# The first layer of a fused four-layer graph network: edge pieces and their products a turn apart, degree sums and first x tile ahead of turn 0

## What is computed

```python
h = maximum(layernorm(x), 0)
x = x + L0(h, W, adj, bias)   # diag, triu, tril of adj, each with its own W[k]
h = maximum(layernorm(x), 0)
x = x + L1(h, adj, ...)       # A_norm = adj + I; dinv = rsqrt(row + column sums - diagonal)
...                           # A_hat = A_norm * dinv[:, None] * dinv[None, :]
x = x + L2(...)               # two graph convolutions and LSTMs over windows
x = x + L3(h, ..., adj, src, dst)   # attention over 256 edges
```

## Time and profile before

| | |
|---|---|
| median of 3 runs | 1282.31 us |
| the profiled execution | 1282.6 us |
| its span | 1280.9 us |
| stage_first within the span | 0 to about 193 us |
| PE busy, share of the span | 95% |
| DVE, ACT, POOL busy | 79%, 68%, 26% |
| mean granted clock of PE | 0.993 |

### The profile page before, as it was taken

How to read it: one execution, slowest core, us unless ns; L and a number is a source line. 1 busy time by engine, 2 the same in 40 slices (tenths; PEclk the granted TensorE clock), 3 DMA queues, 4 the chain that set the end, 5 groups by cost and what they waited for, 6 DMA issues and landing times.

```text
span 1280.9 us, 22499 instructions
## 1 busy us (share of the span) xinstructions
PE 1223.2 (95%) x7286; PEld 1017.2 (79%) x7286; DVE 1013.9 (79%) x2032; ACT 870.9 (68%) x1657; POOL 333.9 (26%) x738
## 2 busy tenths in 40 slices
PE   4888999999899998899999999999999899999998
PEld 4888996663398887689778887888898777778998
DVE  4786868987768885988788878887886699988664
ACT  4564768868668886877687768777776577773332
POOL 4775761000067440000000000000000466653331
PEclk9998999999999999999999999999999999999999
DMA  8000000000031110000000000000200300001212
GB/s 307 1 1 2 2 1 1 0 1 0 19 122 66 66 58 1 1 1 2 1 1 1 1 1 1 1 1 27 105 2 1 132 1 1 2 1 41 75 67 83
DMA packets 14635, 38.22 MB, mean 30 GB/s; under 512 B 1872, under 2 KB 3920, under 8 KB 13392
## 3 DMA queue, kind: packets, MB, share of 16 engines
q1 hardware_dynamic: 13152, 36.31, 7.3%
q10 hardware_dynamic: 1392, 0.74, 0.2%
HBM read 20.27 MB, written 16.78 MB: 29 GB/s over the span
## 4 chain that ended last, share of the span: by engine, by line
PE 52%; DVE 5%; ACT 2%; issue 1%; POOL 1%; POOLq 0%; DVEq 0%; ACTq 0%
PE bank L1091 7%; PE bank L1092 7%; PE bank L1093 7%; PE bank L1563 4%; PE bank L1106 4%; PE bank L1357 4%; PE bank L1102 4%; PE bank L1103 4%; PE bank L1345 4%; PE bank L1553 2%; PE bank L1571 2%; ACT gates L1121 1%; PE bank L1329 1%; PE bank L1247 1%; DVE Y L1176 1%
## 5 line engine op out<-in xcount | busy, mean ns | idle before, releaser
L1121 ACT ACTIVATE gates<-bank,lstm_bias 128x512 f32<-128x512 f32 (+1 forms) x504 | 301.6, 636 | 102.1 <-PE bank L1106 89.2
L161 ACT ACTIVATE l_h<-X,nmr,rstd 128x128 f32<-128x128 f32 (+1 forms) x512 | 209.9, 483 | 38.6 <-POOLq L155 25.9
L1091 PE MATMUL bank<-lstm_node_hi,Wih_hi 128*128 128x512 f32 (+1 forms) x408 | 149.4, 366 | 0.0
L1092 PE MATMUL bank<-lstm_node_hi,Wih_lo 128*128 128x512 f32 (+1 forms) x408 | 148.9, 365 | 0.0
L1093 PE MATMUL bank<-lstm_node_lo,Wih_hi 128*128 128x512 f32 (+1 forms) x408 | 148.9, 365 | 0.0
L130 POOL TENSOR_TENSOR l2r_sum<-l2r_st 128x8 f32<-128x8 f32 x16 | 4.2, 263 | 529.1 <-DVE l2r_st L111 529.1
L1102 PE MATMUL bank<-lstm_hid_hi,Whh_hi 128*128 128x512 f32 (+1 forms) x288 | 104.5, 363 | 4.0 <-DVE lstm_hid_hi L1181 3.8
L1106 PE MATMUL bank<-lstm_hid_lo,Whh_hi 128*128 128x512 f32 (+1 forms) x288 | 106.9, 371 | 0.0
L1103 PE MATMUL bank<-lstm_hid_hi,Whh_lo 128*128 128x512 f32 (+1 forms) x288 | 103.2, 358 | 0.0
L1126 ACT ACTIVATE gates<-lstm_cell 128x512 f32<-128x512 f32 (+1 forms) x144 | 83.7, 581 | 20.8 <-DVE lstm_cell L1168 20.5
L1093 PEld LDWEIGHTS bank<-lstm_node_lo,Wih_hi 128*128 128x128 f32 x408 | 77.1, 189 | 11.6
(11 more groups left out here) (248 smaller groups left out, 3275.4 us busy)
## 6 DMA issues: line engine op xcount, KB each, us to landing
x_spill<-X SPq DMA_DIRECT2D x32, 256.0 KB, 2.0
X<-x_spill SPq DMA_DIRECT2D x2, 4096.0 KB, 12.6
out<-X SPq DMA_DIRECT2D x32, 256.0 KB, 2.0
X<-in_x SPq DMA_DIRECT2D x7, 1024.0 KB, 16.1
X<-in_x SPq DMA_DIRECT2D x2, 512.0 KB, 7.2
w_raw<-in_WihT SPq DMA_DIRECT2D x1, 1024.0 KB, 6.1
w_raw<-in_WhhT SPq DMA_DIRECT2D x1, 1024.0 KB, 8.3
W<-in_L_W ACTq DMA_DIRECT2D x1, 192.0 KB, 3.0
```

The costliest lines, as they stand in the source:

```text
L161: last = act.activation(h[:, j, :], k.X[:, bass.ds(b0, TB), :][:, j, :], ACT.Relu, bias=k.nmr[:, bass.ds(b0, TB)][:, j:j + 1], scale=k.rst ...
L1091: pe.matmul(out, hi, x_high, start=True, stop=False)
L1092: pe.matmul(out, lo, x_high, start=False, stop=False)
L1121: act.activation(gate_of(it, g), k.bank[4 * s + g][:, 0:it.N], ACT.Tanh if g == GATE_G else ACT.Sigmoid, bias=k.lstm_bias[:, it.p - 1, g:g ...
```

## The change

- **Edge pieces and products.** The constants change so that a full turn lies between each piece and its product: the scaled identity in behind(0) and the spread in turn 2; perm stays in behind(6) and the sort goes to turn 8; ST and DT in behind(8) and the adjacency product in turn 10; the three products behind it move by two turns as well. Copying the edge lists to float moves from turn 4 to turn 2 (READ), the rounded copy of DT to turn 9 (ROUND). PT, the four operations on Wqv and a_sign, and cont with reset are gathered behind turn 14 (REST).
- **Degree sums.** The seven DVE operations (L442 to L451) move from the end of turn 0 to a place ahead of turn 0; the pow for dinv on POOL moves from its turn 1 to a place between the coefficients of turns 0 and 1.
- **x first.** adj and adjT go to ACT's queue, ahead of the row vectors and W0; cols, W1T, W2T and Wg go from ACT's queue to SP's, behind x and the edge lists. x comes in pieces of 1, 1, 2, 2, 2 tiles and then six of 4.
- **First tile alone.** Turn 0's coefficients are made in two batches of one tile (4 columns) in place of one of 8; the counts that later waits look for grow by one.
- **Start of PE.** 8 dummy matmuls go before the diagonal product and 16 behind it; the waits for the split adjacency, for W0 and for the diagonal move from ahead of turn 0 into it, in front of their first use.

```diff
@@ LayerNormTail @@
     def wait(self, eng, s, turn):
-        eng.wait_ge(self.ready[s // self.per], turn + 1)
+        eng.wait_ge(self.ready[s // self.per], turn + 1 + (self.first_alone and (turn > 0 or s == 1)))
...
+    def coefficients_alone(self, pool, s):
+        self.batch(pool, 0, 0, s)
...
+        late = self.first_alone and (alone is None or alone == 1)
+        base = (turn * self.batches + q + late) * self.GROUPS
...
@@ stage_first @@
-    turns_in = [1, 1] + [2] * ((n_it - 2) // 2)
+    tiles_in = [1, 1, 2, 2, 2] + [4] * ((tiles - 8) // 4)
...
-    DEG, SPREAD, L3, FLOAT, RANK, PERM, SORTED, ADJ, SUM, TURN, SHARE = 0, 3, 3, 4, 5, 6, 7, 8, 9, 10, 11
+    SCALE, SPREAD, READ, FLOAT, RANK, PERM, SORTED, ROUND, ADJ, SUM, TURN, SHARE, REST = 0, 2, 2, 4, 5, 6, 8, 9, 10, 11, 12, 13, 14
@@ sync @@
-            sp.dma_start(adj[:, :], d["adj"]).then_inc(adj_in, 16)
-            sp.dma_start(k.adjT[:, :], d["adjT"]).then_inc(adj_in, 16)
...
+            sp.dma_start(k.cols[:, :], d["cols"]).then_inc(cols_in, 16)
+            sp.dma_start(k.W1T[:, :], d["W1T"]).then_inc(w_in, 16)
...
@@ gpsimd @@
-            x_ln.coefficients(pool, 0)
+            for s in range(S):
+                x_ln.coefficients_alone(pool, s)
+            pool.wait_ge(deg, 4)
+            pool.tensor_tensor(out=dinv[:, :], in0=rs[:, 3:4], in1=k.ln_const["-half"][:, 0:1], op=ALU.pow).then_inc(dinv_p, 1)
+            x_ln.coefficients(pool, 1)
             pool.iota(order_row[:, :], ...)
...
-            x_ln.coefficients(pool, 1)
@@ scalar @@
+            act.dma_start(adj[:, :], d["adj"]).then_inc(adj_in, 16)
+            act.dma_start(k.adjT[:, :], d["adjT"]).then_inc(adj_in, 16)
+            act.dma_start(k.rows[:, :, :], d["rows"].partition_broadcast(P)).then_inc(rows_in, 16)
             act.dma_start(W0[:, :, :], d["L0_W"].rearrange("k f o -> f k o")).then_inc(w0_in, 16)
...
-                if i == FLOAT:
+                if i == READ:
...
-                if i == ADJ:
+                if i == ROUND:
@@ tensor @@
             pe.wait_ge(cst, 2)
+            stay_awake(pe, k, psA[0], 8)
             pe.wait_ge(diag_in, 1)
             pe.matmul(spare[:, 0:P], k.ones[:, :], tmp[:, :], start=True, stop=True).then_inc(diag_done, 1)
-            pe.wait_ge(A_ready, 2)
-            pe.wait_ge(w0_in, 16)
+            stay_awake(pe, k, psA[0], 16)
...
@@ vector @@
-                if i == DEG:
...
-                if i == SPREAD - 1:
+                if i == SCALE:
...
-                if i == L3:
+                if i == REST:
+                    dve.tensor_tensor(e.PT[:, :], ST[:, :].bitcast(F32), DT[:, :], ALU.add)
                     dve.wait_ge(l3_in, 3 * 16)
...
-                    dve.wait_ge(matched, 2)
-                    dve.tensor_tensor(e.PT[:, :], ST[:, :].bitcast(F32), DT[:, :], ALU.add)
-                if i == SUM:
+                if i == REST:
                     chained(dve.memset(cont[:, :], 0.0))
...
-            x_stats(0)
+            x_stats(0, [0])
             dve.wait_ge(masks, 2)
             split_float32(dve, A12T[:, :, :], A_hi[:, :, :], A_lo[:, :, :], A_ready, 1).then_inc(A_ready, 1)
             dve.wait_ge(diag_done, 1)
             dve.tensor_copy(diag_bc[:, :], spare[:, 0:P]).then_inc(diag_done, 1)
-            x_stats(1)
-            for s in range(S):
-                h_low(0, s)
+            x_stats(0, [1])
+            degrees()
+            x_stats(1, [0])
+            h_low(0, 0)
+            x_stats(1, [1])
+            h_low(0, 1)
```

More of the change, by code:

```diff
@@ L118, in coefficients, with batch @@
             self.batch(pool, turn, q)
-    def batch(self, pool, turn, q):
+    def coefficients_alone(self, pool, s):
+        self.batch(pool, 0, 0, s)
+    def batch(self, pool, turn, q, alone=None):
         k, c = self.k, self.k.ln_const
[L122 to L126, removed]
+        whole, first = self.per * self.nb, (alone or 0) * self.nb
+        width = whole if alone is None else self.nb
+        st6 = self.st6[:, q * whole + first:q * whole + first + width, :]
+        su, di, m2 = self.sum[:, 0:width], self.diff[:, 0:width], self.m2[:, 0:width]
+        late = self.first_alone and (alone is None or alone == 1)
+        base = (turn * self.batches + q + late) * self.GROUPS
+        rows = bass.ds((turn * self.batches + q) * whole + first, width)
         rstd, nmr = k.rstd[:, rows], k.nmr[:, rows]
@@ L134, in group @@
             pool.sem_inc(self.tally, 1)
-        for s in range(q * self.per, (q + 1) * self.per):
+        for s in range(q * self.per, (q + 1) * self.per) if alone is None else [alone]:
             pool.wait_ge(self.stats_ready[s], turn + 1)
@@ L142, in batch @@
         group(1)
-        pool.sem_inc(self.stats_free[q], 1)
+        if alone is None or alone == self.per - 1:
+            pool.sem_inc(self.stats_free[q], 1)
         tt(di, di, di, ALU.mult)
@@ L197, in stage_first @@
     tile = lambda i, s: X[:, (i * S + s) * TB:(i * S + s + 1) * TB, :]
-    turns_in = [1, 1] + [2] * ((n_it - 2) // 2)
-    x_in = each(len(turns_in), lambda c: sem(f"x_in{c}"))
-    chunk_of = [c for c, n in enumerate(turns_in) for _ in range(n)]
+    tiles_in = [1, 1, 2, 2, 2] + [4] * ((tiles - 8) // 4)
+    x_in = each(len(tiles_in), lambda c: sem(f"x_in{c}"))
+    chunk_of = [c for c, n in enumerate(tiles_in) for _ in range(n)]
     adj_in, w0_in, w_in, rows_in, cols_in, edges_in, l3_in = (
@@ L234, in _ @@
         def _(sp):
-            sp.dma_start(adj[:, :], d["adj"]).then_inc(adj_in, 16)
-            sp.dma_start(k.adjT[:, :], d["adjT"]).then_inc(adj_in, 16)
             first = 0
-            for c, n in enumerate(turns_in):
-                rows = slice(first * S * TB, (first + n) * S * TB)
+            for c, n in enumerate(tiles_in):
+                rows = slice(first * TB, (first + n) * TB)
                 sp.dma_start(X[:, rows, :], d["x"][:, rows, :]).then_inc(x_in[c], 16)
@@ L245, in _ @@
                 sp.dma_start(col_i[:, n, :], d[name + "_col"]).then_inc(edges_in, 16)
+            sp.dma_start(k.cols[:, :], d["cols"]).then_inc(cols_in, 16)
+            sp.dma_start(k.W1T[:, :], d["W1T"]).then_inc(w_in, 16)
+            sp.dma_start(k.W2T[:, :, :], d["W2T"].rearrange("(h c) o -> c h o", h=2)).then_inc(w_in, 16)
+            sp.dma_start(k.Wg[:, 0, :], d["Wg0"]).then_inc(w_in, 16)
+            sp.dma_start(k.Wg[:, 1, :], d["Wg1"]).then_inc(w_in, 16)
             sp.dma_start(e.Wqv[:, :], d["Wqv"]).then_inc(l3_in, 16)
@@ L391, in _ @@
                 extra_read(i)
+                if i == 0:
+                    pe.wait_ge(w0_in, 16)
+                    pe.wait_ge(diag_done, 2)
                 for s in range(S):
```

43 lines of the change are left out of this document (19 added, 24 removed).

## The result

The changed kernel takes 1267.6 us (median of five executions) against 1282.3. The ratio is 0.9876 with a 95% interval of 0.9864 to 0.9889, so it is 1.2% faster, and the forecast was 1267.5. One of the five executions took 1745.1 us at a granted clock of 0.65, which nothing here explains; the ratio leaves it out, and the other four lie between 1266.2 and 1267.9 (median 1267.0, that is 15.4 us less instead of 14.7).

What follows compares the result with a forecast made beforehand. TensorE was busy 95% of the span, but POOL's 10.0 us a turn would bind in stage_first once the holes went. Gain 19.0 - 2.65 - 1.6 = 14.8 us, so 1267.5 us against 1282.3, range 1261 to 1274.

Steps and rivals of the forecast that it cites:

- Start: Beginning of stage_first: x's statistics at 4.7 us, normalise(0) at 9.5, normalise(1) at 19.0 against 23.67, 4.7 us gained.
- The second path: Start: PE and ScalarE, from slot 1's normalise through its products and copies, reach normalise(1) at 18.6 to 19.5 us.
- Dummies at nothing: Start: the 25 dummy and diagonal matmuls lie in time in which PE waited 11.4 us anyway, costing nothing.
- The holes: PE's waits ahead of three products: 10.1 us of holes and 5 to 6 us of slow clock go.
- POOL needs 10.0: Turns of stage_first: POOL's two coefficient batches take 10.0 us a turn, so turns can't fall to PE's 9.10.
- DVE pieces in the turns at nothing: Pieces of 0.3 to 1.1 us lie in the 0.9 us PE waits each turn; cost nothing, 0.5 us at most.
- A clock of 1.00 from turn 1 to 14: Sign that the forecast is right: PE's granted clock stays at 1.00 through these turns of stage_first.
- A slower POOL: Rival: one more stretched POOL operation in each of 26 batches, 10.4 us more, 1277.9 us; chance 0.12.
- REST: Pieces behind turn 14 delay the last turn's Z0 by 2.65 us; slow clock behind the hole costs 1.6 us more.
- Sum: Whole gain in stage_first: 19.0 - 2.65 - 1.6 = 14.8 us.
- move as a block: Everything behind stage_first has the same instructions and only shifts earlier together.

Runs made afterwards that it cites:

- e8: Changed kernel with the loads back in the old order and on the old queues, x's first pieces kept at one tile: 1270.5 us.
- e4: Kernel before with only the wider spacing between DVE pieces and their products, nothing gathered behind turn 14: 1268.8 us.
- e6: Changed kernel with turn 0's coefficients in one batch of 8 columns again, first tile's statistics still taken alone: 1271.1 us.
- e7: Changed kernel without the 8 and 16 dummy matmuls at the start: 1267.5 us.
- e2: Changed kernel with the pow of every LayerNorm coefficient batch replaced by a multiplication, so rstd is another number: 1257.9 us.
- e3: Changed kernel's start alone (loads, first tile, degree sums, dummies), with the turns' constants of the kernel before: 1276.6 us.
- e1: Changed kernel with the three pieces gathered behind turn 14 spread over turns 7, 9 and 12: 1265.3 us.
- e9: Changed kernel with 12 dummy matmuls ahead of PE's wait for Z0 in the last turn: 1265.6 us.
- e5: Changed kernel with degree sums back behind turn 0, dinv behind POOL's turn 1 batches, scaled identity behind turn 2, spread in turn 4: 1270.1 us.

## Why the prediction was right, step by step

- **Start.** Statistics at 4.7 forecast, 5.04 measured; normalise(0) 9.5 and 9.83, its second slot 13.3 and 13.58, normalise(1) 19.0 and 19.45. The 0.3 us at the beginning is most of it: DVE awaits both adjacency loads first, and the second landed at 4.8 where it had at 3.95 before the change. Why is open; with the old order of the loads it landed at 5.2 in e8 and at 6.0 in e4. The four-column pow took 1.0 as worked out. What the prediction didn't say is by which path the first tile gains: it let POOL's batch for turn 1 start as soon as POOL was free, and e6 shows that DVE's program order counts too. Turn 1's statistics stand behind h_low of slot 0, so an early normalise(0) is what lets POOL go on. The second path that it named, over PE and ScalarE, came out level with POOL's: the batch ended at 19.24, and normalise(1) at 19.45 shows no wait for POOL.
- **Dummies at nothing**: right (e7), also in what they bring.
- **The holes.** "POOL needs 10.0" was the step that decided. The chain of 26 batches was put at 131.2 us and took 131.9; e2 and e4 confirm it, one by taking the bound away, the other by meeting it without the new start. Holes and slow clock together were 15 to 16 us; 13.6 (with the 0.7 of dinv in it) to 14.0 of them came through, the rest went into waits for POOL. e3 shows the other side: start and spacing are worth 7.2 and 14.0 us alone, 21.2 in all, but together, with what REST gives back added (4.25), 17.8. Of the 3.4 us between them, 2.7 have the size of the degree sums and the spread's slow clock (1.3 and 1.4 in e3), which are worth nothing once POOL is behind; that is a sum, and no run shows it by itself.
- **DVE pieces in the turns at nothing**: right in the end, but the size of PE's waits was off: not 0.9 us in every turn, but 1.56 and 1.77 behind FLOAT and RANK and hardly any elsewhere.
- **A clock of 1.00 from turn 1 to 14**: wrong. Behind the wait of 1.77 us it fell at about 78.2 us and cost 1.6 us in that turn. It cost the end nothing: in e7, where it stayed up behind the same wait, from normalise(1) to normalise(15) it is 139.39 us against 139.55, as POOL sets the pace.
- **A slower POOL**: out. Its small operations were stretched, some to 0.64 and 0.79 us as in the last x batch above, but over 26 batches the mean is 5.07 us against the 5.05 put down.
- **REST**: 2.65 and 1.6 forecast (the three rows add up to 2.63), 2.62 and 1.63 measured (e1, e9).
- **Sum.** The stage gained 13.6 us, not 14.8: 0.45 at normalise(1), 0.7 over the 26 batches. The rest of the program, which was to move as a block, took 1086.1 us instead of 1087.7. With the same instructions it took between 1085.8 and 1090.2 in the profiled executions whose batch is unchanged. So 1 to 2 us of the agreement of the median with the forecast is luck; the terms are right within 1.2.

## What to carry to other kernels

When one engine is busy 95% of the time, its waits are not all that can be had back: add up the period of each other engine's chain per turn, because the stalls that are to be removed may be what keeps a slower one in step. Work that must be done somewhere belongs in the turns that wait for another engine, not behind the last but one, where nothing covers it. When a transfer or a tile is moved ahead, follow the program order of the engine that does the next step; there it may wait behind a step of the old order.

## What the runs showed of the hardware

- The granted clock isn't told by the length of a hole. A hole of 3.36 us ahead of the spread brought it down in the kernel before (0.50 at 52 us) and left it at 1.00 in e3. A wait of 1.77 us behind turn 6 brought it down in the changed kernel and in e9, and not in e1, e5, e7 and e8, where turn 6 to 7 took 11.1 us instead of 12.8. The 3.2 us in the last turn brought it down in all five executions that had it, in three of them for the first product behind the hole and in two 0.8 and 1.5 us later, and the 2.35 us there in e2 did not.

```profile
74.16:85.30 11.14, 9.37 (x82) 9.17 (x81) 10.33 (x35) 6.63 (x15) 8.56 (x23) 1.00 0.00 0
```

(Turn 6 to 7 of e7, in the columns of the earlier trace rows; the same turn of the changed kernel stands in the result. The wait for Z0 in it is 1.77 us in both.)

- The first rows of the granted clock can't be relied on: in e7 the column says 1.00 for 12 to 14 us (the line below), while a product takes 0.41 us, as it does in the changed kernel from 14 to 15 us, where the column says 0.50. It seems to show 1.00 until the first change is recorded; the length of the matmuls tells more.

```profile
12.00:14.00 2.00, 1.64 (x8) 1.27 (x7) 1.48 (x5) 0.56 (x2) 1.62 (x4) 1.00 1.02 416
```

(e7, in the columns of the earlier trace rows.)

- The pow on POOL took 1.64 us for 8 columns, 1.0 for 4 and 0.55 for 1, while the other operations took 0.2 us whether for 4 columns or for 8, where they were not stretched. Halving the width so saves 0.6 us of pow. Whole batches: 4.31 us for 8 columns (turn 0 in e6), 3.66 and 3.48 for 4 (the changed kernel).
